# The end of a recurrence and the layer norm behind it, re-ordered over four engines

## The chip, the cores and the metric

The kernel runs on one core of a Trainium2 chip. The metric is the device time of one execution in microseconds (us), as the median of several executions; lower is better. TensorE (PE) does matrix products, VectorE (DVE) and ScalarE (ACT) elementwise work and reductions, GpSimd (POOL) elementwise work on SBUF, and SyncE (SP) starts most DMAs. Each engine works through its own list of instructions in order and waits on semaphores.

## The reference, cut to what matters

The input x has 2048 tokens of width 128. Two blocks follow each other; in each, attention and a feed-forward part read the same layer norm and are added to x.

```python
xn = layernorm(x)
x = x + L0_attn(xn) + L0_ffn(xn)
xn = layernorm(x)                       # the "second norm" of this text
x = x + L1_attn(xn) + L1_ffn(xn)

# L0_attn, F = 64
k, v = phi(k_proj(rmsnorm(xn))), v_proj(rmsnorm(xn))     # phi(z) = elu(z) + 1
for t in tokens:                                          # a recurrence over a 64x128 state M
    M = layernorm_of_matrix(M + eta * norm(v_t - k_t @ M) * outer(k_t, v_t))
out = phi(q_proj(rmsnorm(xn))) @ M @ Wout.T               # only the last M is used

# L0_ffn: expert 1 of the experts, relu(x W1 + b1) W2 + b2
# L1_attn: one head of width 128, the first 64 of them rotated by cos and sin tables, causal softmax
# L1_ffn: ternary weights; silu(x w1) * (x w2), two gelu layers of 512, and w3
```

## The kernel before

The program is written engine by engine; the order on each engine is the order of its code, and every dependence between engines is a semaphore.

**The chain.** The recurrence is cut into 128 lanes of 16 tokens, which start from an assumed state and run 28 steps (the `for j in range(L)` of the VectorE program, L = 28). A step is some seven short VectorE instructions, with a square root on ScalarE in the middle of it (`HS`, then `surprise(j + 1)`). Under it TensorE builds the rest of the first block's output in PSUM banks 0 to 3 (`expert_output(c)` for four blocks of 512 tokens), ScalarE makes copies at fixed steps (`BEHIND_COPY`, `HIDDEN_AT`, `LAST_AT`), and from step 18 VectorE finishes one of the 16 pieces of phi(q) per step (`query_sums`).

**The end of the chain.** TensorE picks a column of the factors (`gcol_done`), VectorE scales the last rows (`UW`), TensorE forms the state times Wout (`mw_done`), ScalarE copies it (`MW`), and `memory_output` adds phi(q) times it to banks 0 to 3. Its last product on a bank raises `ao_done`. Beside this a check compares the end of each lane with the start of the next: `c0` and `c1`, a product that shifts `c0` by one lane, a subtraction, a sum of absolute values, `agree`, a product that counts the lanes that agree, and `flag`. All engines then wait for the flag, load it and branch (`general_path`); a loop over all tokens would follow if lanes did not agree, which is not the case with these inputs.

**The second norm.** It goes by blocks c of 512 tokens. ScalarE copies a block out of PSUM (`first_block`), VectorE takes statistics and variances (block 0 straight from PSUM), ScalarE the square root (`deviations`), VectorE the reciprocal (`shifts`), each of the two normalizes two of the four tiles (`normed`), TensorE transposes (`normed`) and ScalarE copies the result to `xT` (`transposed`). Then `projected` multiplies it with three weights: one to rotate, one swapped, one to skip. VectorE multiplies the first two with the cos and sin tables and adds the halves of the queries; GpSimd adds those of the keys; ScalarE copies the skipped part. The tables are loaded by SyncE, behind a wait for `x1_ready`, into the place of `HT`, which the first block's expert uses until then.

**Behind it** come attention and the gated layer together, tile after tile, then two layers of fp16 products on TensorE, and the stores.

## Time and profile before

| | |
|---|---|
| median of 3 executions | 257.17 us (257.16 to 257.2) |
| the profiled execution | 257.23 us |
| its span, first to last instruction | 255.4 us |
| busy in it | TensorE 244.6, VectorE 204.6, ScalarE 186.1, GpSimd 115.2 us |
| mean granted TensorE clock | 0.997 of full speed |

A time in a row counts from the start of the span. A row of the timeline gives start, duration, engine, line, operation and shapes; neighbours of one line are merged ("x4"), and then the duration is that of the whole run. Durations of neighbours overlap, since an instruction's latency is part of it; the distance between two starts is what it costs the engine. In square brackets stands how long the engine had been idle, and what ended that. "L755" is line 755 of the kernel.

### The profile page before, as it was taken

The page shows a single profiled execution, that of the slowest core. Times are in us where ns is not written, and L with a number is a line of the kernel's source. Part 1 is how long each engine was busy: PE and PEld are TensorE (multiplying, and loading weights), DVE is VectorE, ACT ScalarE, POOL GpSimd, SP SyncE. Part 2 cuts the span into 40 slices and gives each one's busy share as a digit, 9 for nine tenths or more (in the row PEclk, how much of TensorE's full clock was granted, in tenths as well). Part 3 has the DMA queues.
Part 4 walks back from the last instruction along what each step waited for, and adds up shares of the span by engine and source line. Part 5 has one row for each costly group of instructions (what it writes and reads, how often), then busy time and mean ns, then how long its engine had stood idle before and what let it go on. Part 6 is the DMA issues. An engine that isn't in the chain of part 4 may idle for free.

```text
span 255.4 us, 5146 instructions
## 1 busy us (share of the span) xinstructions
PE 244.6 (96%) x1669; PEld 159.9 (63%) x1673; DVE 204.6 (80%) x681; ACT 186.1 (73%) x460; POOL 115.2 (45%) x150
## 2 busy tenths in 40 slices
PE   7899998999998999999999999999999999999993
PEld 2358554776763477787777767886875444444492
DVE  5988799999968998998899887787613996666674
ACT  2597789976637887887767899989814997777720
POOL 9689700000004589887755995987790000000000
PEclk9999999999999999999999999999999999999998
DMA  7720000000007403000000000000000000000014
GB/s 194 209 54 3 1 3 0 1 0 3 3 3 305 190 13 154 3 1 0 4 0 3 0 0 3 1 1 3 1 3 0 0 0 0 3 1 0 1 31 138
DMA packets 8303, 8.50 MB, mean 33 GB/s; under 512 B 1745, under 2 KB 7378, under 8 KB 7762
## 3 DMA queue, kind: packets, MB, share of 16 engines
q1 hardware_dynamic: 7442, 7.65, 9.2%
q10 hardware_dynamic: 832, 0.49, 0.7%
q8 instruction: 15, 0.25, 0.4%
q14 instruction: 14, 0.11, 0.1%
HBM read 7.09 MB, written 1.05 MB: 32 GB/s over the span
## 4 chain that ended last, share of the span: by engine, by line
PE 65%; DVE 19%; POOL 6%; ACT 3%; issue 3%; DMA 2%; DVEq 0%; SPq 0%; POOLq 0%; ACTq 0%
PE PS L954 11%; PE PS L953 11%; PE PS L926 8%; PE PS L903 7%; PE PS L916 4%; POOL arena L1492 3%; POOL arena L1493 3%; PE PS L715 3%; PE PS L669 2%; PE PS L723 2%; DVE mxb L2016 2%; DMA x<-L_attn_x 2%; DVE arena L2002 2%; PE PS L534 2%; PE PS L572 2%
## 5 line engine op out<-in xcount | busy, mean ns | idle before, releaser
L953 PE MATMUL PS<-arena 128*128 128x512 f16 x128 | 48.5, 379 | 0.0
L954 PE MATMUL PS<-arena 128*128 128x512 f16 x128 | 48.5, 379 | 0.0
L2074 DVE TENSOR_TENSOR arena<-arena 128x512 f32<-128x512 f32 x32 | 22.2, 692 | 13.0 <-ACT arena L1411 13.0
L903 PE MATMUL PS<-arena 128*128 128x512 f32 (+3 forms) x80 | 31.9, 530 | 0.3 <-ACT arena L1380 0.3
L1410 ACT ACTIVATE arena<-PS,arena 128x512 f32<-128x512 f32 x32 | 22.9, 716 | 9.1 <-PE PS L954 9.1
L1492 POOL TENSOR_TENSOR arena<-arena 128x256 f32<-128x256 f32 x32 | 21.6, 674 | 15.5 <-DVE arena L2008 13.0
L1380 ACT ACTIVATE arena<-PS,lnt 128x512 f32<-128x512 f32 (+3 forms) x40 | 24.8, 628 | 2.9 <-DVE lnt L2023 2.8
L1493 POOL TENSOR_TENSOR arena<-arena,small 128x256 f16<-128x256 f32 (+1 forms) x36 | 23.8, 662 | 2.8
L1500 POOL CAST arena<-arena 128x512 f16<-128x512 f32 x2 | 1.3, 636 | 49.1 <-ACT x L1273 49.1
L1411 ACT ACTIVATE arena<-PS,arena 128x512 f16<-128x512 f32 x32 | 22.8, 713 | 0.0
L2016 DVE TENSOR_REDUCE mxb<-PS 128x1 f32<-128x512 f32 (+3 forms) x40 | 22.1, 602 | 0.0
L954 PEld LDWEIGHTS PS<-arena 128*128 128x128 f16 x128 | 12.5, 98 | 14.7
L953 PEld LDWEIGHTS PS<-arena 128*128 128x128 f16 x128 | 12.5, 98 | 14.6
L903 PEld LDWEIGHTS PS<-arena 128*128 128x128 f32 x80 | 14.0, 191 | 12.0 <-issue 9.8
L916 PE MATMUL PS<-con,arena 128*128 128x128 f32 x136 | 19.5, 273 | 0.0
L926 PE MATMUL PS<-arena,xn 128*128 128x128 f32 x144 | 19.3, 278 | 0.0
L926 PEld LDWEIGHTS PS<-arena,xn 128*128 128x128 f32 x144 | 17.7, 191 | 1.1 <-ACT xn L1364 0.2
L926 PE MATMUL PS<-arena 128*128 128x128 f32 x128 | 17.3, 278 | 0.6 <-ACT arena L1364 0.6
L916 PEld LDWEIGHTS PS<-con,arena 128*128 128x128 f32 x136 | 15.1, 141 | 2.7 <-issue 1.9
L2045 DVE SCALAR_TENSOR_TENSOR x<-PS,lnt,x 128x128 f32<-128x128 f32 x16 | 5.6, 351 | 13.9 <-PE PS L926 13.6
L926 PEld LDWEIGHTS PS<-arena 128*128 128x128 f32 x128 | 15.6, 191 | 1.3 <-ACT arena L1364 1.0
L2002 DVE SCALAR_TENSOR_TENSOR arena<-PS,arena 128x256 f32<-128x256 f32 x32 | 15.5, 484 | 1.1
(292 smaller groups left out, 614.3 us busy)
## 6 DMA issues: line engine op xcount, KB each, us to landing
arena<-h_T SPq DMA_DIRECT2D x2, 1024.0 KB, 6.0
x<-L_attn_x SPq DMA_DIRECT2D x4, 256.0 KB, 4.7
arena<-cos SPq DMA_DIRECT2D x1, 1024.0 KB, 4.8
arena<-sin SPq DMA_DIRECT2D x1, 1024.0 KB, 6.9
arena<-w_T SPq DMA_DIRECT2D x3, 256.0 KB, 3.0
out<-arena SPq DMA_DIRECT2D x2, 256.0 KB, 2.2
con<-shape_constants ACTq DMA_DIRECT2D x1, 192.5 KB, 3.5
out<-arena SPq DMA_DIRECT2D x1, 192.0 KB, 2.0
```

What stands on the lines that cost most here:

```text
L903: i = mm(PS[:, k, 0:cnt * P], qT1[:, t * P:(t + 1) * P], kT1[:, c * P:(c + cnt) * P], start=True, stop=not last)
L916: i = tr(PS[:, 4 + gi % 2, (b - c) * P:(b - c + 1) * P], Pr[t % 2][:, b * P:(b + 1) * P], ident)
L926: i = mm(PS[:, 7, (t % 4) * D:(t % 4 + 1) * D], PT[t % 2][:, b * P:(b + 1) * P], V1[:, b, :], start=(b == 0), stop=(b == t))
L953: mm(bank(b), wH[:, k, m * P:(m + 1) * P], sH[:, k, cols], start=(k == 0), stop=False)
L954: i = mm(bank(b), wL[:, k, m * P:(m + 1) * P], sL[:, k, cols], start=False, stop=(k == HT4 - 1))
L1380: f(Pr[t % 2][:, c * P:(c + cnt) * P], PS[:, SCORE_BANK[gi], 0:cnt * P], ACT.Exp, scale=1.0 / D, bias=nbs[:, t:t + 1], accum_out=rsums[:, ...
L1410: f(FP[u % 4], bank(u % 8), ACT.Gelu, scale=s_[:, u % HT4:u % HT4 + 1])
L1411: f(high, bank(u % 8), ACT.Gelu, scale=s_[:, u % HT4:u % HT4 + 1]).then_inc(read, 1)
L1492: o.need(o.did(tt(rest, value, high, ALU.subtract)))
L1493: return tt(low, rest, low_scale.broadcast_to([P, cols]), ALU.mult)
L2016: i = did(v.tensor_reduce(mxb[:, gi:gi + 1], PS[:, SCORE_BANK[gi], 0:cnt * P], AX.X, ALU.max))
L2074: v.tensor_tensor(RP[m], FP[m], high, ALU.subtract).then_inc(rest_ready, 1)
```

## The change

1. *Tables.* cos and sin get places of their own. SyncE starts cos when ScalarE has copied the lanes (`lanes_act` 10), sin when the tables of the chain are built; both stand in its queue ahead of the wait for block 3. The buffers `TURN` move to another place.
2. *Last rows.* `LAST_AT` goes from 15 to 16, and the copy of `WVO` moves from behind the chain to step 19.
3. *The check's first part.* At step 13 VectorE takes a reciprocal and at step 18 it forms twelve columns of `c0`; TensorE shifts them before `expert_output(3)`. The `query_sums` at steps 18 to 26 become eight at steps 19 to 26.
4. *End of the chain.* TensorE no longer runs `keep_warm(4)` at step 25. The check's VectorE instructions come right behind `UW`, and the count product goes ahead of all of `memory_output`.
5. *The last half of the queries.* phi(q) is now min(exp(q), 1) + relu(q). For the second half the two terms are not added; VectorE only clips (`query_steps`, two instructions of 256 columns), and TensorE multiplies each term: 16 products where there were 8.
6. *Second norm.* VectorE takes half the statistics of block c + 1 ahead of `shifts(c)`, and `rotated(0)` ahead of `shifts(3)`. ScalarE's order of `first_block`, `deviations`, `normed`, `transposed` and `skipped` is new: `first_block(2)` comes ahead of `deviations(0)`. TensorE transposes block c + 1 inside `projected(c)`, and a transposition starts when its own tile is ready. GpSimd's addition for the keys starts when VectorE's for the queries is done.
7. *Smaller moves.* Five small VectorE instructions on the scales go from behind the norm to before the chain; ScalarE's copies of the masks go ahead of the branch; `keep_warm` behind the output goes from 4 and 7 products to 2 and none.

```diff
-            sp.wait_ge(x1_ready, 2)
-            for i, n in enumerate(("cos", "sin")):
-                sp.dma_start((cosT, sinT)[i], a[n]).then_inc(tab_in, 16)
+            sp.wait_ge(lanes_act, 10)
+            sp.dma_start(cosT, a["cos"]).then_inc(tab_in, 16)
+            sp.wait_ge(tables_ready, 1)
+            sp.wait_ge(terms_act, 2)
+            sp.dma_start(sinT, a["sin"]).then_inc(tab_in, 16)
...
             def memory_output(two, first, end):
-                    pe.wait_ge(q_ready, 2 * (4 * two + k + 1))
+                    pe.wait_ge(q_ready, 9 + k // 2 if two else 2 * (k + 1))
+                    if two:
+                        for c in (2, 3):
+                            mm(PS[:, c, k * P:(k + 1) * P], QE[h0:h0 + F, part], MW[h0:h0 + F, :], start=False, stop=False)
...
-            for j in range(FAR + 1, L):
-                if j in EO_AT:
-                    expert_output(EO_AT.index(j) + 1)
-                elif EO_AT[-1] + 4 < j < L - 2:
-                    keep_warm(4, 4)
+            for k, j in enumerate(EO_AT):
+                if j == EO_AT[-1]:
+                    pe.wait_ge(c0_ready, 1)
+                    mm(PS[0:W, 5, HALF:HALF + REST], ..., c0[0:W - 1, 0:REST], ...).then_inc(shift_done, 1)
+                expert_output(k + 1)
...
+            pe.wait_ge(guard_ready, 2)
+            mm(PS[0:1, 5, 1:2], agree, ...).then_inc(count_done, 1)
             pe.wait_ge(mw_act, 1)
             memory_output(0, 0, 2)
-            pe.wait_ge(agree_ready, 1)
-            mm(PS[0:1, 5, 1:2], agree, ...).then_inc(count_done, 1)
             memory_output(0, 2, 4)
             memory_output(1, 0, 4)
-            keep_warm(4, 4)
+            keep_warm(2, 4)
             general_path(pe, general)
-            keep_warm(7, 4)
...
+            first_block(1)        # ScalarE
+            first_block(2)
+            deviations(0)
+            first_block(0)
+            normed(0)
+            transposed(0)
+            deviations(1)
+            normed(1)
+            first_block(3)
+            deviations(2)
+            transposed(1)
+            normed(2)
+            deviations(3)
+            skipped(0)
+            transposed(2)
+            normed(3)
+            skipped(1)
+            transposed(3)
...
             for c in range(4):    # GpSimd
-                pool.wait_ge(rope_dve, 2 * c + 2)
+                pool.wait_ge(turned_dve, c + 1)
...
-            query_sums(9, 10)
+            query_steps(0)
             (reciprocal, c0, c1, UW, subtraction, sum, agree)
-            query_sums(11, 12, 13, 14, 15)
+            query_steps(1)
             (flag)
...
             for c in range(4):    # VectorE
+                if c < 3:
+                    statistics(c + 1, 0)
+                else:
+                    rotated(0)
                 shifts(c)
                 normed(c)
                 if c < 3:
-                    statistics(c + 1)
+                    statistics(c + 1, 1)
                     variances(c + 1)
+            rotary_sum(0)
+            rotated(1)
+            rotary_sum(1)
+            for c in range(2, 4):
+                rotated(c)
+                rotary_sum(c)
```

## Rows read from the trace of the kernel before

**Rows 1.** Busy time of each engine by stage; (x) counts instructions.
```profile
core 0: us, PE busy (x) PEld busy (x) DVE busy (x) ACT busy (x) POOL busy (x), PEclk, DMA share, GB/s
...
94.00:115.00 21.00, 20.77 (x152) 16.47 (x152) 18.95 (x54) 16.79 (x49) 18.56 (x24) 1.00 0.15 51
...
133.00:250.00 117.00, 116.59 (x747) 75.58 (x748) 84.78 (x190) 88.46 (x181) 46.72 (x52) 1.00 0.01 4
```

**Rows 2.** Chain that ended last, 71 to 81 us: start, duration, what.
```profile
71.11 0.30 DVE arena L1860
...
73.39 0.16 DVE flag L1876
...
74.70 0.90 DVE st L1933 x4
...
76.04 0.30 ACT lnt L1279
...
79.90 0.79 DVE st L1940 x4
```

**Rows 3.** Timeline of TensorE.
```profile
69.94 0.81 PE L510 MATMUL PS<-warm 128*128 128x512 bf16 x3
70.68 0.28 PE L769 MATMUL PS<-con,arena 128*32 128x1 f32 x4
...
72.52 0.71 PE L755 MATMUL PS<-arena 64*128 64x128 f32 x8 [0.20 <-ACT arena L1253]
...
73.28 1.61 PE L755 MATMUL PS<-arena 64*128 64x128 f32 x24
...
77.78 0.66 PE L825 MATMUL PS<-con,xn 128*128 128x128 f32 x4 [0.41 <-ACT xn L1286]
...
79.52 1.12 PE L834 MATMUL PS<-xT,arena 128*128 128x512 f32 x2 [0.21 <-ACT xT L1290]
80.48 1.02 PE L835 MATMUL PS<-xT,arena 128*128 128x512 f32 x2
...
91.94 1.05 PE L850 MATMUL PS<-arena,xT 128*128 128x128 f32 x8
```

**Rows 4.** Timeline of VectorE.
```profile
27.89 0.19 DVE L1675 TENSOR_TENSOR arena<-arena 128x28 f32<-128x28 f32 x1 [1.24 <-ACT arena L1142]
...
59.44 0.20 DVE L1788 TENSOR_TENSOR_SCAN arena<-arena 128x18 f32<-128x18 f32 x1 [0.18 <-ACT arena L1234]
...
76.37 0.18 DVE L1951 RECIPROCAL lnt<-lnt 128x4 f32<-128x4 f32 x1 [0.36 <-ACT lnt L1279]
...
79.01 0.18 DVE L1951 RECIPROCAL lnt<-lnt 128x4 f32<-128x4 f32 x1 [0.36 <-ACT lnt L1279]
...
84.71 0.16 DVE L1968 TENSOR_SCALAR arena<-arena 128x4 f32<-128x4 f32 x1
...
85.18 0.68 DVE L1982 TENSOR_TENSOR arena<-PS,arena 128x512 f32<-128x512 f32 x1
...
92.61 0.69 DVE L1986 TENSOR_TENSOR arena<-arena 64x512 f32<-64x512 f32 x1
```

**Rows 5.** Two lines of GpSimd: count, duration ns min/median/max, first and last start.
```profile
L1507 POOL TENSOR_TENSOR arena<-arena x4: 1701/1773/1778, 86.6 to 92.7; 64x512 f32<-64x512 f32 x4
...
L1492 POOL TENSOR_TENSOR arena<-xT,arena x4: 1156/1156/1161, 94.6 to 101.8; 128x512 f32<-128x512 f32 x4
```

**Rows 6.** Timeline of ScalarE, in the chain and at the softmax's start.
```profile
58.55 0.22 ACT L1184 ACTIVATE arena<-PS 32x64 f32<-32x64 f32 x1 [0.96 <-PE PS L747]
...
69.53 0.40 ACT L1234 ACTIVATE arena<-arena 128x6 f32<-128x6 f32 x1
...
94.01 0.37 ACT L1380 ACTIVATE arena<-PS,lnt 128x128 f32<-128x128 f32 x1
```

**Rows 7.** The line of the table loads (SyncE's queue).
```profile
L449 SPq DMA_DIRECT2D arena<-sin x1: 433/433/433, 77.2 to 77.2; - x1
...
DMA to landing us min/median/max: 4.8/5.8/6.9
```

**Rows 8.** TensorE's work, granted clock and DMA at the end (columns of rows 1).
```profile
254.00:255.40 1.40, 0.00 (x0) 0.00 (x0) 0.00 (x0) 0.00 (x0) 0.00 (x0) 0.50 0.03 9
```

More of the change, by code:

```diff
@@ L241, in program @@
         assert max(b_at[0], at[0]) <= 44992, (b_at, at)
-        TURN = [hBf[:, T * c:T * c + 2 * BANK].rearrange("p (k t) -> p k t", k=2) for c in range(2)]
+        TURN = [hAf[:, 2 * T + 2 * BANK * c:2 * T + 2 * BANK * (c + 1)].rearrange("p (k t) -> p k t", k=2) for c in range(2)]
         xd = hBf[:, T + 2 * BANK:T + 3 * BANK]
@@ L753, in memory_output @@
                     for c in (2 * two, 2 * two + 1):
                         h0 = F * (c % 2)
-                        i = mm(PS[:, c, k * P:(k + 1) * P], QT[h0:h0 + F, (4 * two + k) * P:(4 * two + k + 1) * P], MW[h0:h0 + F, :], start=False, stop=(k == 3))
+                        i = mm(PS[:, c, k * P:(k + 1) * P], QT[h0:h0 + F, part], MW[h0:h0 + F, :], start=False, stop=(k == 3))
                         if k == 3:
                             i.then_inc(ao_done, 1)
-            for j in range(FAR + 1, L):
+            for k, j in enumerate(EO_AT):
@@ L859, in _ @@
                 projected(c)
-                for n in ((2,), (3,), (), ())[c]:
-                    normed(n)
             values(0)
@@ L1294, in high, with skipped @@
                 f(xH[:, c * BANK:(c + 1) * BANK], xT[:, c * BANK:(c + 1) * BANK], ACT.Copy).then_inc(xh_act, 1)
-            first_block(1)
-            deviations(0)
-            first_block(0)
-            normed(0)
-            first_block(2)
-            deviations(1)
-            transposed(0)
-            first_block(3)
-            normed(1)
-            deviations(2)
-            normed(2)
-            transposed(1)
-            deviations(3)
-            normed(3)
-            transposed(2)
-            f(small[:, 38:39], lnt[:, 0, 12:13], ACT.Tanh)
-            for c in range(4):
+            def skipped(c):
                 b = 4 * ((c + 1) % 2)
@@ L1736, in query_sums @@
                     part = slice(q * P // 2, (q + 1) * P // 2)
-                    v.scalar_tensor_tensor(out=QT[:, part], in0=QE[:, part], scalar=1.0, in1=QT[:, part], op0=ALU.min, op1=ALU.max).then_inc(q_ready, 1)
+                    v.scalar_tensor_tensor(out=QT[:, part], in0=QE[:, part], scalar=1.0, in1=QT[:, part], op0=ALU.min, op1=ALU.add).then_inc(q_ready, 1)
             formed = added = o.n
@@ L1828, in _ @@
                     mean_terms(linear)
+                    dve.wait_ge(h_ready, REST)
+                    v.reciprocal(rh[:, 0:1], HS[:, REST:REST + 1]).then_inc(rh_ready, 1)
                     dve.wait_ge(far_done, FAR)
@@ L1853, in _, with query_steps @@
                     formed = mean_terms(formed)
-            query_sums(9, 10)
+            def query_steps(h):
+                part = slice(BANK + h * ZC, BANK + (h + 1) * ZC)
+                v.tensor_scalar(QE[:, part], QE[:, part], 1.0, None, ALU.min).then_inc(q_ready, 1)
+            query_steps(0)
             dve.wait_ge(h_ready, L)
-            v.reciprocal(rh, HS[:, REST:L + 1:HALF]).then_inc(rh_ready, 1)
+            v.reciprocal(rh[:, 1:2], HS[:, L:L + 1]).then_inc(rh_ready, 1)
+            dve.wait_ge(rh_ready, 2)
@@ L1934, in first_variances, with statistics @@
                 variances(0)
-            def statistics(b):
-                dve.wait_ge(x1_ready, b if b == 1 else b + 1)
-                for n in range(4 * b, 4 * b + 4):
+            def statistics(b, half):
+                dve.wait_ge(x1_ready, (1, 2, 4)[b - 1])
+                for n in range(4 * b + 2 * half, 4 * b + 2 * half + 2):
                     did(v.bn_stats(st[:, n, :], x[:, n, :]))
```

117 lines of the change are left out of this document (62 added, 55 removed).

## The prediction

> **What bounds the kernel now.** I read the chain of waits first: up to 70 us it runs through the recurrence, then through the flag and the second norm, then through GpSimd and VectorE in the attention, and from 132 us through TensorE alone. The busy times by stage [rows 1] say the same. From 133 to 250 us TensorE works 116.59 of 117 us, and nothing there is edited. From 94 to 115 us TensorE (20.77 of 21) and GpSimd (18.56) are both nearly full. So the question is how much earlier the work at 94 us can start. Then I read the timelines of 53 to 98 us, engine by engine.
>
> From 70 to 76 us four waits follow each other [rows 2]: UW at 71.11, `memory_output` at 72.52 [rows 3], the flag at 73.39, and 1.31 us later the first statistics at 74.70, though TensorE had finished block 0 before. Those 1.31 us are VectorE's load of the flag and its branch. The square root of block 0 is at 76.04. From 76.37 to the last rotary addition at 92.61 + 0.69 = 93.30 the path stays on VectorE, with idle times of 0.36 us before the reciprocals of blocks 1 to 3 [rows 4] (the second and third repeat the one at 79.01). TensorE's projections run from 79.52 to 91.94 without a gap [rows 3], a second limit close behind. GpSimd's last addition starts at 92.7 and takes 1.77 [rows 5], to 94.43.
>
> **The change, part by part.**
>
> *Tables.* The load of sin starts at 77.2 and lands 6.9 us later [rows 7], at 84.1. Before, that is hidden, since the first product with a table is at 85.18 [rows 4]. Moved alone it is worth nothing, but `rotated(0)` comes at about 82.5 after the change and would wait 1.6 us without it. The new loads start at about 30 and 34 us and have 40 us of cover. In SyncE's queue they stand ahead of the load of h1 alone, which is not delayed by them. I cost their writes under the chain at 0: VectorE's run of four statistics takes its usual 0.79 us at 79.90 [rows 2], under the old load of sin. Bounds 0 to +0.2 us.
>
> *Scales.* Five instructions from 84.71 to 85.18 leave the path, 0.47 us. Their new place is VectorE's idle 1.24 us before 27.89 [rows 4]; their loads stand at the head of SyncE's queue. Cost there 0; without that cover 0.47.
>
> *In the chain.* ScalarE idles 0.96 us before 58.55 for the last rows [rows 6] and so takes the square root of step 16 some 0.3 us late; VectorE idles 0.18 before the scan at 59.44, step 17 [rows 4]. One step later the rows are there: −0.18. The reciprocal at step 13 costs +0.05 to +0.1, the distance between two such small starts. At step 18 the c0 product takes the place of a query piece. Sum −0.13, bounds −0.2 to +0.2.
>
> *End of the chain.* TensorE runs three recorded warm products from 69.94 and reaches the column pick at 70.68 [rows 3], while its factors were ready at 69.53 + 0.40 = 69.93 [rows 6]. Without them, and with the shift product (0.2 us) ahead of `expert_output(3)`, it picks at about 70.2. VectorE now has a clipping, a reciprocal, c0 and c1 ahead of UW, some 0.8 us behind the last scan, so UW moves only from 71.11 to about 70.8. `memory_output` follows 1.41 us behind UW as before (72.52 − 71.11), at 72.2. The check runs right behind UW: three instructions at some 0.2 us (short ones take 0.16 to 0.22 [rows 4, 6]), agreement at 71.6, count at 71.7, flag at 71.95, released engines at 73.25. `memory_output(0)` is 16 records: eight took 0.71 and 24 took 1.61 us [rows 3], so a record costs about 0.06 and 16 with their tail 1.15. Banks 0 and 1 are ready at 73.4, and the statistics of block 0 start there, 1.3 us earlier.
>
> *Two products.* The second half is 32 records instead of 16, about +0.95 us. Banks 2 and 3 are ready at 72.2 + 47 × 0.0575 + 0.27 = 75.2, where they were ready at 73.28 + 1.61 = 74.89. What does this delay? ScalarE's `first_block(2)` waits for it, and `deviations(0)`, ready at 74.7, is queued behind that wait. The copy costs ScalarE 0.5 us, so the square root runs at 75.8 instead of 76.04 [rows 2]. **Of the 1.3 us gained at the flag only 0.24 are left.** Bounds: records at 0.067 us (1.61 / 24) give 75.65 + 0.6 = 76.25, that is +0.2; 0.4 is the most on the other side.
>
> *Second norm on VectorE.* Before: 93.30 − 76.37 = 16.93 us. Off it go the three idle times (1.08), the scales (0.47) and half the statistics of block 1, done ahead (0.4). I walked both engines forward with durations of these rows and found new idle times: 0.1 for the copy of block 0, 0.23 for the square root of block 1, 0.12 for the copy of block 3. Result 15.43, that is −1.5. Bounds −0.8 (each interleave half filled) and −1.9.
>
> *TensorE.* Block 0's transposition ends at 77.75 instead of 78.44 (ScalarE is not on block 2 then), the copy to xT runs at once instead of behind block 2 and a square root, and the first projection starts at 78.6 instead of 79.52. Twelve projections and three transpositions follow as before, where they filled the 12.42 us from 79.52 to 91.94 (some 0.6 us for a transposition, 0.88 for a product [rows 3]). In my walk ScalarE's copies hold them up by little, and they end at 90.35 instead of 91.94, −1.6. VectorE's last rotation needs the swap of block 3 at 89.5 and comes just then.
>
> *GpSimd.* The old additions take 1.70 to 1.78 us on 64 x 512; a subtraction of 128 x 512 takes 1.16 [rows 5]. The old ones start together with VectorE's addition of two SBUF inputs (0.69 us) and the difference is 0.6. Now they start behind it, beside products that read PSUM. I take 1.16: start 0.65 later, 0.6 shorter, no net cost, and the last ends at 91.55 + 1.2 = 92.75 instead of 94.43, −1.7. The other bound is 1.77 again, which leaves −1.1.
>
> The Trainium skill (GPSIMD Engine Reference, Specifications) says that GpSimd's SBUF interfaces are shared with VectorE and contend with VectorE instructions that have two SBUF inputs. The trace agrees with 1.77 against 1.16. By the rule this wait costs nothing; without it the key additions would end 0.6 later.
>
> *Masks, warm products.* The masks (0.3 us each) lie behind MW's copy and end at 72.6, before ScalarE is released. The fewer warm products save nothing on the path, as TensorE waits until 77.78 anyway [rows 3]; they leave it idle for about 1.3 us at 75.7 to 77.0, where the gap was 0.41.
>
> **Sum at the start of the attention.** VectorE: −0.24 − 1.5 = −1.75. TensorE −1.6. GpSimd −1.7. ScalarE, with both `high` copies now ahead of the first exponential (94.01 [rows 6]), −1.2; it is the least full in the stage that follows (16.79 of 21 us [rows 1]), which takes this up. Everything behind is unedited, so I take the smallest of the three that are full: −1.6. The profiled execution took 257.23, the median 257.17. 257.2 − 1.6 = **255.6 us**.
>
> **Rivals.**
>
> *A. The head of ScalarE's queue costs more.* `first_block(2)` is ready late (76.25 for the square root), and the new idle times on VectorE double. Then −0.2 becomes +0.2, −1.5 becomes −1.0: 257.2 − 0.8 = 256.4. For it speaks that one wait holds all four blocks; against it that even then VectorE has a half block of statistics to fill each gap.
>
> *B. The gain is kept in full and more.* If the c = 0 path through the flag, the shorter chain and the transpositions by tile each reach their better bound, TensorE starts 2.3 us earlier: 254.9.
>
> *C. Attention takes the gain back.* It begins with ScalarE 1.2 early only, or with GpSimd at its other bound (−1.1), and what is full is decided by that one: 257.2 − 0.6 to 1.1, or nothing if another engine's order holds it. About 256.7 to 257.2. Against it: all three start together, and no transfer or fixed time stands in between.
>
> *D. Slower: the clock.* The granted clock is 1.00 in every stage [rows 1] but behind the work: 254 to 255.4 us, without one product and behind others without any, has 0.50, that is 1.2 GHz [rows 8]. The kernel after idles 1.3 us at 75.7 and waits in pieces from 71 to 72.2. If the clock fell there, the projections behind it would take 1.7 us each instead of 0.86. It decides from about two of them on (1.6 us lost); six would give 257.2 − 1.6 + 5.2 = 260.8. Against it: 0.41 us of idle time left the clock at 1.00, and the only fall stands behind a longer stretch without work than this change makes.
>
> The Trainium skill (Advanced Engine Details and Errata, Clock Domains) says that the array is gated to 1.2 GHz when idle. The trace agrees at its end only; no stage before it shows such a fall.
>
> *E. The chain gets longer.* Table writes (+0.2) and the two instructions in it (+0.2), and A on top: 257.3 to 257.5.
>
> **Chances and range.** My forecast with its own range of 255.1 to 256.1: 0.58. A: 0.14. B: 0.08. C: 0.10. D: 0.04. E: 0.06. A measurement of this kernel can tell 0.2%, 0.5 us, from no change. Faster than 256.66: forecast, A, B and a fifth of C, 0.82. Same: most of C and half of E, 0.11. Slower: D and half of E, 0.07. The range from 254.8 to 256.7 takes in A and B and leaves out some 0.18.
>
> **What would show it.** In the profile after: UW near 70.8 and the flag near 71.95; L755's counterpart with 48 records, ending near 75.2; ScalarE's second 512-column copy waiting for it, and the first square root behind that, near 75.8; idle before VectorE's reciprocals under 0.25; the last rotary addition ending near 91.5; GpSimd's key additions at about 1.2 us; TensorE's value products starting near 90.4; granted clock 1.00. It is wrong if a projection stands at a half clock, if the chain's last scan comes later than 70.0, or if the softmax starts 1.6 us earlier and the end does not.

## The result, and the profile after

The kernel after took **260.56 us** (median of 4 executions, 259.16 to 260.63), the kernel before on the same chip 257.17 (257.11 to 257.2): a ratio of 1.0116, 95% interval 1.0103 to 1.013. The change makes the kernel 3.4 us slower where 1.6 us less was forecast. The profiled execution took 260.58 us, its span is 258.8 us.

First the windows of the kernel after around the end of the chain (the columns are start and end, length, busy time and count of each engine, granted clock, DMA share, GB/s):

```profile
core 0: us, PE busy (x) PEld busy (x) DVE busy (x) ACT busy (x) POOL busy (x), PEclk, DMA share, GB/s
...
71.00:72.60 1.60, 1.23 (x8) 0.90 (x8) 1.35 (x9) 0.57 (x3) 0.00 (x0) 1.00 0.00 0
72.60:73.00 0.40, 0.37 (x4) 0.38 (x6) 0.00 (x0) 0.37 (x2) 0.00 (x0) 0.76 0.00 0
73.00:76.00 3.00, 3.00 (x32) 3.00 (x30) 1.36 (x10) 0.60 (x1) 0.00 (x0) 0.50 0.00 0
...
79.00:80.00 1.00, 0.00 (x0) 0.00 (x0) 0.97 (x8) 0.41 (x2) 0.00 (x0) 0.82 0.00 0
80.00:83.00 3.00, 2.57 (x8) 1.81 (x10) 1.10 (x7) 1.13 (x3) 0.00 (x0) 0.50 0.02 5
```

The clock stands at 0.50, that is 1.2 GHz, from 73 to 76 us, in the middle of a stretch in which TensorE is busy 3.00 of 3.00 us, and again from 80 to 83. Before each fall TensorE had worked in pieces (1.23 of 1.60 us) or not at all (79 to 80). The pieces alone don't tell a fall: the kernel before works 1.26 us between 71 and 72.6 and stays at 1.00. The timeline of TensorE in the kernel after:

```profile
70.43 0.28 PE L777 MATMUL PS<-con,arena 128*32 128x1 f32 x4 [0.17 <-ACT arena L1239]
...
72.63 1.95 PE L762 MATMUL PS<-arena 64*128 64x128 f32 x16 [0.27 <-ACT arena L1259]
74.36 0.64 PE L759 MATMUL PS<-arena 64*128 64x128 f32 x4
...
76.81 0.39 PE L762 MATMUL PS<-arena 64*128 64x128 f32 x4
77.36 0.38 PE L512 MATMUL PS<-warm 128*128 128x512 bf16 x1 [0.16 <-issue]
80.21 1.11 PE L832 MATMUL PS<-con,xn 128*128 128x128 f32 x4 [2.47 <-issue]
81.55 1.49 PE L512 MATMUL PS<-warm 128*128 128x512 bf16 x3 [0.22 <-issue]
82.83 1.14 PE L841 MATMUL PS<-xT,arena 128*128 128x512 f32 x2
```

L762 and L759 are `memory_output`. Its 48 records (the trace shows two for a product in f32) run from 72.63 to 77.2, 4.6 us, where 3.0 were forecast: a group of four costs 0.43 us at the half clock and 0.22 at the full one (76.59 to 76.81). Then comes the second surprise. The transposition of block 0 starts at 80.21, and what ended TensorE's 2.47 us of idle time is "issue": no other engine. Behind the product at 77.36 stands the branch around the general path of the recurrence. The profile lists the branch under its own line, one row per engine; first the kernel before, then the kernel after:

```profile
L486 PEldq COMPARE_BRANCH  x1: 367/367/367, 74.7 to 74.7; - x1
```

```profile
L488 PEldq COMPARE_BRANCH  x1: 3617/3617/3617, 76.5 to 76.5; - x1
```

The same instruction, taken the same way, takes TensorE 0.37 us before and 3.62 us after. DMA traffic from 70 to 84 us, by queue (packets, MB, share), again before and then after:

```profile
q8 instruction: 1, 0.02, 0.4%
```

```profile
q8 instruction: 2, 0.03, 1.0%
```

Queue 8 carries code in pieces of 16 KB, and it is TensorE's: two kernels below that lengthen TensorE's program alone (e2, f1) have 16 pieces on it in their traces, where these two have 15. In both kernels a piece starts 1.1 us behind the start of the branch, at 75.9 us before and 77.6 after. The next one comes at 89.8 us before and already at 80.9 after, 0.7 us behind the end of the long branch. In the kernel after nothing but code moves between 70 and 84 us, so no other transfer can be in the way.

VectorE and ScalarE in the kernel after, against [rows 2, 4]:

```profile
70.38 0.20 DVE L1804 TENSOR_TENSOR_SCAN arena<-arena 128x18 f32<-128x18 f32 x1
...
71.29 0.28 DVE L1890 TENSOR_SCALAR arena<-arena,PS 64x128 f32<-64x128 f32 x1
...
72.39 0.15 DVE L1901 TENSOR_SCALAR flag<-PS 1x1 int32<-1x1 f32 x1
74.60 0.89 DVE L1958 BATCH_NORM_STATS2 st<-PS 128x6 f32<-128x128 f32 x4 [2.06 <-PE PS L762]
...
78.05 0.18 DVE L1976 RECIPROCAL lnt<-lnt 128x4 f32<-128x4 f32 x1 [1.77 <-ACT lnt L1287]
...
82.18 0.18 DVE L1976 RECIPROCAL lnt<-lnt 128x4 f32<-128x4 f32 x1 [1.86 <-ACT lnt L1287]
```

```profile
77.23 0.60 ACT L1281 ACTIVATE x<-PS 128x512 f32<-128x512 f32 x1 [1.99 <-PE PS L762]
77.73 0.29 ACT L1287 ACTIVATE lnt<-mv,small 128x4 f32<-128x4 f32 x1
```

ScalarE's copy of bank 2 does wait for the doubled products, and the first square root is queued behind it, at 77.73 instead of the forecast 75.8. The last scan of the chain comes at 70.38; it was at 70.03 before. The update of the first tile of the attention is at 99.95 where it was at 96.78, 3.2 us late, and nothing behind gives this back.

### The profile page after: what moved, and what is told of

It is laid out like the page before. It is cut to its first block, busy times and chain, and to the rows that moved or that the text cites. A ratio compares the mean times of both kernels' runs of the same rounds, so it can differ in the third digit from the quotient of the medians.

```text
span 258.8 us, 5147 instructions
## 1 busy us (share of the span) xinstructions
PE 245.1 (95%) x1674; PEld 162.0 (63%) x1678; DVE 204.4 (79%) x676; ACT 185.8 (72%) x460; POOL 113.0 (44%) x150
## 4 chain that ended last, share of the span: by engine, by line
PE 66%; DVE 24%; ACT 3%; issue 3%; DMA 2%; SPq 0%; DVEq 0%; ACTq 0%
PE PS L958 11%; PE PS L959 11%; PE PS L931 9%; PE PS L908 9%; PE PS L921 5%; DVE arena L1785 3%; DVE arena L2036 2%; DVE arena L1772 2%; DVE arena L2035 2%; DVE arena L1804 2%; DMA x<-L_attn_x 2%; DVE mxb L2050 2%; DVE arena L1813 2%; DVE arena L1873 2%; PE PS L882 2%
## 5 line engine op out<-in xcount | busy, mean ns | idle before, releaser
L1373 ACT ACTIVATE xn<-PS 128x512 f32<-128x512 f32 (+1 forms) x20 | 10.4, 551 | 8.4 <-PE PS L921 8.4
```

## The experiments

Sixteen kernels ran, in four sets; each ratio is against the kernel before on the same chip. A position in TensorE's program, in the text below, is that in each kernel's compiled program, labels left out: a product in f32 is four instructions (the trace shows two products in f32 as x4, and as many weight loads), any other two; a wait is part of the instruction behind it or one of its own, and two waits in a row share one. Where the loaded program begins is not known, so only the distances between kernels count. The expectations count from the kernel's text instead, each wait as one, which gives higher numbers: there the kernel before has the target of its first branch at 1669 and its last branch at 4500, here at 1440 and 3739.

**First set: the clock or the branch?**

*e1.* Warm products put back in the chain.

```diff
+            pe.wait_ge(scan_ready, L - 2)
+            keep_warm(4, 4)
             pe.wait_ge(wvo_act, 1)
```

> The changed kernel with the four warm products back behind expert_output(3) (they ran at step 25 of the chain before). Theory 1 (the first fall of the clock, at 72.6 us, comes from TensorE having too little to do from 70.25 on, because these four are gone): granted clock 1.00 from 72 to 76 us; the 48 records of memory_output take about 2.9 instead of 4.6 us, though they start 0.4 to 0.6 us later; the branch of TensorE (3.6 us in the changed kernel) and the gap behind it stay, and the second fall at 79.5 may stay. About 259.2 us. Rival (the two products per tile of the second half are slow by themselves, whatever the clock): the records stay at 0.1 us and the time is 260.6 or more.

258.82 us (257.21 to 259.59), ratio 1.005 (1.0028 to 1.0072). In the profiled execution (259.53) the clock is 1.00 from 72.6 to 76 and `memory_output` takes 2.95 us as forecast. The branch still takes 3.39 us, and TensorE is idle 2.51 us on "issue". The clock then falls behind it. So four products are enough against the first fall, and it isn't all. Three of the ten executions took 257.21 to 257.43 us at a clock of 0.998 to 1.00; no trace of one is kept.

*e2.* The kernel after with its branch later in the program, by 32 waits, fulfilled already, behind each of two `expert_output`s. These 64 waits were meant as 64 instructions and are 32, since two share one. The trace has 30 of them under the line itself:

```profile
L775 PEldq EVENT_SEMAPHORE  x30: 51/51/51, 59.9 to 65.1; - x30
```

```diff
                 expert_output(k + 1)
+                if k < 2:
+                    for _ in range(32):
+                        pe.wait_ge(scan_ready, j + 1)
```

> The changed kernel with 64 extra waits that are already fulfilled in TensorE's program, 32 each behind expert_output(1) and (2), where its queue is full of work; they move every later instruction of TensorE by 64 places and do nothing else. Theory 2 (TensorE's branch takes 3.6 us because its target lies outside the code that is already loaded; code comes in pieces of 16 KB in the trace): the branch takes about 0.4 us as before, block 0 is transposed at about 79.3 instead of 80.2, the clock does not fall a second time or later, about 258.5 to 259.5 us. Rival (the branch is long because the slow products ahead of it have to drain, or because of the flag): it stays at 3.6 us and the time at 260.6.

257.71 us (256.21 to 260.13), ratio 1.0007 (0.9979 to 1.0036). The profiled execution is the 260.13 one, the slowest of ten: branch 3.04 us where 0.4 was expected, and the last branch, around the network's general path, now 1.79 us instead of 0.35. Four of ten executions took 256.2 to 256.35 at a clock of 0.997 to 1.00. In the profiled one the clock did not fall at 72.6 although no warm product had been put back; it fell at 78.4, behind the branch. Only adding instructions that do nothing made the median 2.9 us faster.

*e3.* Both edits.

> Both edits of the first two. If both theories hold and nothing else went wrong in the prediction, the clock is 1.00 throughout, the branch 0.4 us, and the time 255.6 to 256.2 us. If the prediction's sum for the interleaved norm was wrong too, it stays above 256.7.

258.08 us (257.34 to 258.31), ratio 1.0028 (1.0018 to 1.0038), clock 1.00 throughout. The branch took 1.82 us, hidden behind the wait for block 0. The first projection is at 79.09 and the value products start at 91.46, 0.48 earlier than [rows 3]. The last branch took 1.39 us, 1.06 more than before. This was the first sight of the change at full clock: it is worth 0.5 us at the attention, not 1.6.

*e4.* The kernel before, with 64 waits more (33 instructions) in the part of the general path that is jumped over. Nothing that is executed changes.

```diff
                 for two in range(2):
                     memory_output(two, 0, 4)
+                for _ in range(64):
+                    pe.wait_ge(gmw_act, 2)
```

> The kernel before, with 64 waits added inside TensorE's general path, which is jumped over, so that the branch has 64 instructions more to jump. Theory 2: the branch takes 3.6 us instead of 0.37, from 74.7 to 78.3, the seven warm products behind it run after that, block 0 is transposed about 1 us or more later, 258 to 259.5 us. Rival: nothing that is executed is changed, 257.2 us.

259.01 us (258.08 to 259.89), ratio 1.0066 (1.0041 to 1.0091): code that is never executed costs the kernel before 1.8 us in the median. Three executions took 258.08 to 258.39 us at a clock of 0.995 to 1.00, so about 1.0 more, and three 259.62 to 259.89 at 0.989 to 0.993. TensorE in the profiled one (259.76), timeline and windows:

```profile
74.82 1.04 PE L510 MATMUL PS<-warm 128*128 128x512 bf16 x3
78.24 2.73 PE L510 MATMUL PS<-warm 128*128 128x512 bf16 x6 [2.39 <-DVE xn L1959]
```

```profile
76.00:78.00 2.00, 0.00 (x0) 0.00 (x0) 1.49 (x9) 1.93 (x5) 0.00 (x0) 1.00 0.23 33
78.00:82.00 4.00, 3.76 (x12) 2.06 (x13) 2.62 (x18) 0.65 (x3) 0.00 (x0) 0.57 0.89 358
```

The branch itself reads 364 ns here, yet the warm products right behind it, which wait for nothing, start at 78.24. The profile gives the idle time to VectorE, for which these products don't wait. The clock falls to 0.57 after this gap, as in the kernel after.

The Trainium skill (Runtime: NRT & Kernel Launch, Instruction fetch mechanics) says that code comes in blocks of 16 KiB, 256 instructions, ahead of need, and that a taken branch to code outside a window of two blocks has to wait for a fetch. The 16 KB pieces on queue 8 and the 1.8 us of this run agree with it; that the branch itself reads 364 ns here, and the stall stands behind it, is not in it.

**Second set: a cleaner move of the branch; the warm products; the norm.**

*f1.* As e2, with 64 waits in each place, so 32 instructions there.

> The changed kernel with 128 fulfilled waits (64 behind expert_output(1), 64 behind (2)) in TensorE's program instead of the 64 of the run before, and no warm products put back. Theory 2 refined (the piece of code with the branch's target is loaded only once TensorE's program has crossed into the piece before it; with 64 waits that crossing came in the middle of the branch, with 73 places just ahead of it and the branch took 1.8 us; the second branch at the end then took 1.4 to 1.8 us instead of 0.33): with another 64 places both crossings come a microsecond or more earlier, and both branches take about 0.4 us. Block 0 is then transposed when its tiles are ready (78 us or sooner). Time 256.4 to 257.2 us where the clock holds; some runs still lose the clock. Rival (the length of the branch has nothing to do with the place of the code): 3 us again.

259.38 us (258.79 to 259.82), ratio 1.0088 (1.0074 to 1.0101). The branch fell to 0.93 us, but TensorE now idles 0.95 us ahead of an `expert_output` and 0.99 ahead of the c0 product, so UW came 1.7 us late: 128 waits cost time that the chain has no room for. The means spoiled the measurement. Both branches were expected at 0.4 us; the last took 1.17.

*f2.* The kernel before without its warm products at step 25.

```diff
-                elif EO_AT[-1] + 4 < j < L - 2:
-                    keep_warm(4, 4)
```

> The kernel before without its four warm products at step 25: the one edit alone. The prediction had the column pick 0.5 us earlier and UW 0.3 to 0.45 earlier, so 256.8 us by it. Theory 1 (they carried the clock): the granted clock falls between 72 and 76 us in some or all runs, and the time is 257.2 to 258.5 or scatters.

257.07 us (256.77 to 257.49), ratio 0.9997 (0.9988 to 1.0006). In time those products are worth nothing to the kernel before. But they carry its clock too: without them the mean clock is 0.989 to 0.992 in seven of eleven executions, and with them it is 0.996 or more in all 15 that ran beside. The profiled execution of f2 (256.93 us) shows the fall where the kernel after has it; the first row is that of its windows, the second that of `memory_output`:

```profile
73.00:76.00 3.00, 3.00 (x26) 2.50 (x27) 1.43 (x10) 0.94 (x3) 0.00 (x0) 0.53 0.03 5
72.90 2.72 PE L755 MATMUL PS<-arena 64*128 64x128 f32 x24
```

These 24 records take 2.72 us where they took 1.61 [rows 3]. It costs little in the end: the seven executions have a median of 257.21 us, the four others 256.91. UW comes 0.38 us earlier without the four products (70.73), and block 0's square root, which in this order stands ahead of the copy of bank 2, comes at 75.66 instead of 76.04 [rows 2] in this execution with the fall.

*f3* is f1 with warm products in the gaps:

```diff
-            keep_warm(1, 4)               # behind the column pick
+            keep_warm(3, 4)
...
+            keep_warm(1, 6)               # behind the count
             pe.wait_ge(mw_act, 1)
             memory_output(0, 0, 2)
...
             general_path(pe, general)
+            keep_warm(5, 4)
```

*f4* is f3 with the second norm in the order of before on all engines.

> The kernel of the first run of this group, with warm products put only where TensorE waits: two more behind the column pick, one behind the count, and five behind the branch. Clock 1.00 throughout, both branches 0.4 us; block 0's square root at 75.9 to 76.3, projections from about 78.7, attention 0.7 to 1.0 us earlier than before. Theory 3 (what the interleaved norm really gives is about 1 us, not 1.6, and attention gives 0.2 to 0.5 of it back): 256.2 to 256.7 us. By the prediction's sum it would be 255.6.

> The kernel of the run before with the second norm in the order of the kernel before on all four engines (GpSimd's wait too), and everything else as changed. It shows what part 6 is worth at full clock. By the prediction the interleave is worth 1.5 us on VectorE, so 1.2 to 1.5 us slower than the run before; by theory 3, with TensorE's projections as the bound, 0.5 to 0.9 us slower.

f3: 259.70 us (259.53 to 259.91), ratio 1.01 (1.0084 to 1.0115). f4: 258.88 us (258.8 to 259.5), ratio 1.0075 (1.0061 to 1.0089). Both miss what was expected. Warm products alone brought f1 nothing, since its clock was already near 1.00. The old order was to lose 0.5 us or more; it won by 0.8, but 0.57 of that is the last branch, which took 0.99 us in f3 and 0.42 in f4. An uncontrolled branch spoils a comparison of two orders too.

**Third set: the jump shortened, without a wait.**

*g1.* The kernel after with three of four `expert_output`s and six of eight groups of `memory_output` taken out of TensorE's general path, which these inputs never run.

```diff
-                for c in range(4):
-                    expert_output(c)
-                for two in range(2):
-                    memory_output(two, 0, 4)
+                expert_output(3)
+                for two in range(2):
+                    memory_output(two, 3, 4)
```

> The kernel after, with most of TensorE's share of the general path of the recurrence taken out (one expert_output instead of four and two of its eight groups of memory_output). These inputs never run that path, so all work that is executed is the kernel after's, and only the length of the code that is jumped over changes. Theory 'code place': TensorE's branch takes 3.6 us in the kernel after because its target lies too far on, and about 0.4 us here; TensorE is then back at 77.6, waits for block 0's normalised rows (79.4) and transposes them there instead of at 80.2, 0.8 us earlier; with the half clock at 72.6 to 76 left (no warm product is put back) the time is about 259.5. Rival 'clock alone': the branch takes as long as before, or its length hides nothing, and the time stays at 260.5.

257.82 us (257.42 to 259.65), ratio 1.0038 (1.0019 to 1.0057): 2.7 us back, without touching an executed instruction. Its two branches, and TensorE in the block stage:

```profile
L488 PEldq COMPARE_BRANCH  x1: 364/364/364, 75.4 to 75.4; - x1
...
L499 PEldq COMPARE_BRANCH  x1: 1030/1030/1030, 250.8 to 250.8; - x1
```

```profile
75.94 0.38 PE L512 MATMUL PS<-warm 128*128 128x512 bf16 x1 [0.16 <-issue]
77.52 0.86 PE L831 MATMUL PS<-con,xn 128*128 128x128 f32 x4 [1.20 <-DVE xn L1981]
78.43 0.81 PE L512 MATMUL PS<-warm 128*128 128x512 bf16 x3
79.08 1.11 PE L840 MATMUL PS<-xT,arena 128*128 128x512 f32 x2
```

TensorE waits for the normalised rows now, as it should. The gap of 1.2 us that I had forecast is there, and the clock stays at 1.00 behind it. I had expected the fall at 72.6 to remain. By the mean clock it did in two of nine executions only (0.987 and 0.988, 259.24 and 259.65 us); the seven others took 257.42 to 258.04, median 257.79. Between 71 and 72.6 us the profiled one works the same 1.23 of 1.60 us as the kernel after, and its clock stays at 1.00. Without the four products the fall there comes in a part of the executions, and costs this kernel 1.65 us when it does. Of the 2.7 us that g1 gains, that much is the clock's, which falls ahead of the branch; why it falls so much less often here than in the kernel after is open.

*g2* adds the warm products of f3, *g3* the old order of the norm on top, *g4* is g2 with one product instead of two for the last half of the queries.

```diff
-                    if two:
-                        for c in (2, 3):
-                            mm(PS[:, c, k * P:(k + 1) * P], QE[h0:h0 + F, part], MW[h0:h0 + F, :], start=False, stop=False)
...
-                v.tensor_scalar(QE[:, part], QE[:, part], 1.0, None, ALU.min).then_inc(q_ready, 1)
+                v.scalar_tensor_tensor(out=QT[:, part], in0=QE[:, part], scalar=1.0, in1=QT[:, part], op0=ALU.min, op1=ALU.add).then_inc(q_ready, 1)
```

> As the run with the short jump, and with warm products in TensorE's gaps: two more behind the column pick, one behind the count, five behind the branch. Theory (clock and code place are the whole loss): UW at 71.3, memory_output at full clock, 2.95 us, statistics at 74.1, first projection at about 78.9, clock 1.00 up to the end: 256.4 to 257.0, at or a little below the kernel before. Rival 'the new order of the second norm is slower too': above 257.3, and the old order (next run) below this one by 0.5 or more.

> As the run before it, but with the second norm in the order of the kernel before on all engines (rotary and key additions too). If the new order is worth what its earlier projections show (about 0.5 us at the attention, nothing behind tile 6): 0.0 to 0.5 us slower than the run with the new order. If the 0.8 us by which the old order won in the earlier pair of kernels belongs to the order: 0.5 to 0.8 us faster. If it belonged to where the code of the last branch lies (0.57 us there): equal within 0.3.

> As the run with the short jump and warm products, but the last half of the queries is again one product: VectorE adds and clips two pieces of 256 columns in the two places where it only clipped, and TensorE's 16 extra records go. Banks 2 and 3 are ready 0.9 us earlier, UW 0.1 to 0.15 and the flag 0.2 later. If first_block(2) is what holds the square root: 0.4 to 0.7 us earlier at the square root, and up to 0.3 us in the end, since TensorE's projections and attention limit what is left: 256.2 to 256.8. Rival: the two products cost nothing in the end, same within 0.2.

g2: 257.61 us (257.27 to 257.99), ratio 1.0017 (1.0008 to 1.0026). g3: 257.38 (257.09 to 257.75), ratio 1.0009 (1.0 to 1.0018). g4: 257.15 (255.36 to 257.58), ratio 0.999 (0.9973 to 1.0006). g2 and g4 missed what was expected of them, and g3 came out as its third case said (equal to g2 within 0.3). For the misses there is one reason: the last branch took 0.87, 1.00 and 1.61 us. When the layers begin, g2 is 0.29, g3 0.56 and g4 1.08 us ahead of the kernel before, and the branch takes that back. Two executions of g4 took 255.36 and 255.42.

Over the kernels so far, the position of the last branch, taken modulo 256, sorts its time (one profiled execution of each; that of e2 is its slowest):

| kernel | position | modulo 256 | last branch, us |
|---|---|---|---|
| f2 | 3732 | 148 | 0.33 |
| before | 3739 | 155 | 0.33 |
| e4 | 3772 | 188 | 0.33 |
| after | 3775 | 191 | 0.35 |
| e1 | 3783 | 199 | 0.34 |
| e2 | 3807 | 223 | 1.79 |
| g4 | 3553 | 225 | 1.61 |
| e3 | 3815 | 231 | 1.39 |
| g1 | 3577 | 249 | 1.03 |
| f1 | 3839 | 255 | 1.17 |
| g2 | 3593 | 9 | 0.87 |
| g3 | 3595 | 11 | 1.00 |
| f3 | 3855 | 15 | 0.99 |
| f4 | 3857 | 17 | 0.42 |

From 148 to 199 it is short. At 223 it is at its longest, and it falls with the distance from there, over the end of the 256, to 0.42 at 17.

**Fourth set: both branches where such branches were short.** The positions were used as a rule, counted from the text as in the expectations: target of the first branch at 1669 or less, last branch just under 4500, that of the kernel before. In the compiled programs this made targets of 1428 to 1434 and last branches at 127 to 145 modulo 256.

*h1.* The kernel after with the warm products of f3, and 64 instructions less to jump over.

```diff
-                for two in range(2):
-                    memory_output(two, 0, 4)
+                memory_output(0, 2, 4)
+                memory_output(1, 3, 4)
```

*h2* is the kernel after with the single product of g4 and nothing else. *h3* is h2 with the warm products, *h4* is h3 with the old order of the norm. In these three the general path is whole: the single product itself takes away 32 instructions ahead of the branch and 32 inside.

> The kernel after with its warm products in TensorE's gaps, and 64 instructions less in the part of the general path that is jumped over (three of TensorE's eight groups of memory_output are left there; these inputs never run that path). So both branches of TensorE lie where they lay in kernels in which they were short: the first one's target 1669 instructions into the program, as in the kernel before, the last branch at 4494 (before: 4500). Theory 'code place': 0.36 us for the first branch and about 0.35 for the last, and 257.61 - 0.5 to 0.6 = 257.0 us. Rival 'something else delays the end': the last branch is short and the time stays at 257.6; rival 'the place in the program as counted says nothing': one of the branches takes 0.9 us or more.

> The kernel after with one product for the last half of the queries, nothing else: no warm product is put back, and the general path is whole. The 32 instructions that go from each of the two groups bring the first branch's target to 1651 and the last branch to 4476. Theory: both branches short, banks 2 and 3 ready 0.9 us earlier: 256.0 to 256.5 if the clock stays at 1.00 from 71 to 80, 257 to 258 if it falls there. Rival: the order and the missing warm products are what costs, above 259.

> As the run with the single product, and with warm products in TensorE's gaps (two more behind the column pick, one behind the count, five behind the branch); a whole kernel. First target at 1669, last branch at 4494. In the run with the short jump the same work stood 1.08 us ahead of the kernel before when the layers began and lost 1.3 of it in the last branch. Theory: 257.15 - 1.2 = 255.9 us, clock 1.00. Rival: the last branch is long here too, 257.1.

> As the run before it, but with the second norm in the order of the kernel before. In the pair with the doubled product the old order was 0.23 us faster. If that belongs to the order: 255.7, 0.2 under the new order. If the new order needs banks 2 and 3 early (it does, ScalarE copies bank 2 second): the new order is now the faster one, by up to 0.5.

| kernel | median, us | range | ratio (interval) |
|---|---|---|---|
| h1 | 257.08 | 256.81 to 257.19 | 0.9997 (0.9988 to 1.0006) |
| h2 | 256.06 | 255.84 to 257.09 | 0.9966 (0.9953 to 0.9978) |
| h3 | 256.19 | 255.92 to 256.25 | 0.9959 (0.9946 to 0.9972) |
| h4 | 256.58 | 256.39 to 256.74 | 0.9978 (0.9969 to 0.9987) |

In all four the first branch took 0.37 us and the last 0.32, as the rule said. h1, h2 and h4 came out as expected; h3 was expected at 255.9. Here is h1 at the branches:

```profile
L488 PEldq COMPARE_BRANCH  x1: 373/373/373, 75.2 to 75.2; - x1
...
L499 PEldq COMPARE_BRANCH  x1: 317/317/317, 250.7 to 250.7; - x1
```

h1 is the whole change at full clock with short branches: no difference to the kernel before. h2 is the fastest version found, with nothing left out, 1.1 us under the kernel before and 4.5 under the kernel after. The warm products bring it nothing in the median (h3 against h2), but h2 has one execution in six at a clock of 0.991 and 257.09 us, and h3 none.

## Why the prediction was wrong

The forecast was −1.6 us. The kernel lost 3.4, and 3.5 lie between it and h1. **The steps that failed are two that I had costed at nothing.**

**The clock ("The fewer warm products save nothing on the path", and rival D at 0.04).** Rival D had the right mechanism and nearly the right total (260.8), with the clock's fall put at the wrong place: I looked at the idle 1.3 us behind `memory_output`. In g1 a wait of 1.2 us stands there and the clock stays at 1.00. The fall came earlier, behind the pieces up to 72.6, and held `memory_output` for 4.6 us instead of 2.95, so 1.65; the two low executions of g1 give the same 1.65 from total times. My argument against it, that 0.41 us of idle time had left the clock alone, spoke of one gap, not of a stretch of small ones. That the products of step 25 carried the clock is shown from both sides: put back, the fall is gone (e1); taken out of the kernel before alone, it comes (f2, 0.53 from 73 to 76 us). There it costs 0.3 us at most. It costs 1.65 in the kernel after, where `memory_output` has twice the records for banks 2 and 3 and the square root of block 0 is queued behind the copy of bank 2; that this is the reason for the difference is argued and not run by itself. What tips a given execution is not settled: g1 and e2 do the same work in their traces and keep the clock.

**The branch (in no term of the sum).** I priced VectorE's branch at 1.31 us and never asked what TensorE's costs, since TensorE waits for ScalarE behind it anyway [rows 3]. The change adds 20 instructions ahead of it and 32 to the path it jumps. It then takes 3.25 us more. Of these, 0.8 lie on the path directly (80.21 against rows ready at 79.4), and the clock that falls behind the idle time adds 1.06: from the transposition to the first projection it is 2.62 us in the kernel after and 1.56 in h1. By total times: the kernel after at 260.58 against g1's two executions with the first fall, 259.45, is 1.13, and g1 pays 0.68 more at its last branch, together 1.8. With the 1.65 above that makes 3.45 of the 3.48 us between the kernel after and h1. That code which is never executed is the cause is shown from both sides, by e4 (+1.8 in the kernel before) and g1 (−1.1 at a like first fall). Both edits change the length of the jump and the place of its target together; which of the two counts they don't separate.

**The rest, at full clock: h1 against the forecast.** TensorE and VectorE in h1:

```profile
71.21 0.28 PE L780 MATMUL PS<-arena,con 128*128 128x1 f32 x2
...
72.65 1.16 PE L762 MATMUL PS<-arena 64*128 64x128 f32 x16
...
77.33 0.86 PE L834 MATMUL PS<-con,xn 128*128 128x128 f32 x4
...
78.89 1.11 PE L843 MATMUL PS<-xT,arena 128*128 128x512 f32 x2
...
91.26 1.05 PE L859 MATMUL PS<-arena,xT 128*128 128x128 f32 x8
```

```profile
70.30 0.20 DVE L1806 TENSOR_TENSOR_SCAN arena<-arena 128x18 f32<-128x18 f32 x1
...
71.21 0.28 DVE L1892 TENSOR_SCALAR arena<-arena,PS 64x128 f32<-64x128 f32 x1
...
73.84 0.89 DVE L1960 BATCH_NORM_STATS2 st<-PS 128x6 f32<-128x128 f32 x4 [1.37 <-PE PS L762]
...
76.44 0.18 DVE L1978 RECIPROCAL lnt<-lnt 128x4 f32<-128x4 f32 x1 [0.93 <-ACT lnt L1289]
...
91.48 0.69 DVE L2002 TENSOR_TENSOR arena<-arena 64x512 f32<-64x512 f32 x1
```

- *Chain.* Forecast −0.13, got +0.27 at the last scan (70.30 against 70.03; +0.35 in the kernel after). The late last rows gave −0.15 at their step, as argued, and the reciprocal cost +0.05. But two steps elsewhere, at 48 and 68 us, lost 0.2 us each, and the cause is open: small transfers of code stand there, but in the kernel before too. Among the h kernels the last scan varies from 70.19 to 70.51 with no edit in the chain.
- *Flag.* UW 71.21 for 70.8 and statistics 73.84 for 73.4: both late by the chain's error. The step itself, flag and statistics ahead of the output, was right: 0.86 us gained over [rows 2].
- *Doubled product.* 2.95 us for the 48 records (3.0 forecast). The square root is at 76.12: +0.08 where −0.24 was forecast and +0.2 was the bound. So it takes the whole gain at the flag. Against the single product it costs 1.0 us in the end (h1 against h2, or 0.9 against h3). The step named the wait rightly, and by the trace at hand a reader could have said that this part should be left out.
- *Second norm on VectorE.* From first reciprocal to the end of the last rotary addition 15.73 us; 16.93 before, 15.43 forecast. The last one ends at 92.17, 1.13 us earlier than before. This walk held.
- *TensorE's projections: the failed walk.* 78.89 to 91.26 is 12.37 us where I walked 11.75; before it was 12.42. [Rows 3] showed this stretch without a gap, so only its start could move, and moving transpositions about inside it could gain nothing. The walk's own prices say the same: 12 × 0.88 + 3 × 0.6 = 12.36, which from 78.6 ends at 90.96 and not 90.35, and the last 0.3 is the start. With the start 0.63 earlier, the attention gets 0.7 and not 1.6. This is the mis-sized term, and it is the one that decides there, since TensorE gains least of the three: GpSimd's last addition ends at 93.52, 0.91 earlier than before.
- *Second norm in all.* The new order against the old one: 0.2 us slower with the doubled product (g2 against g3, although g3's last branch is 0.13 longer), 0.4 faster with the single one (h3, h4). It pays when banks 2 and 3 come early.
- *Tables, scales, masks.* Hidden, as costed.

**What attention gives back (rival C).** Of the 0.7 us at its start h1 has 0.08 left in the end. That is the outcome of rival C, to which I had given 0.10. The first of GpSimd's key additions in the kernel after:

```profile
89.34 1.27 POOL L1516 TENSOR_TENSOR arena<-arena 64x512 f32<-64x512 f32 x1 [1.07 <-DVE arena L2000]
```

1.27 us instead of 1.77 [rows 5], near the bound that I took. All three engines do start earlier in h1, and the updates of tiles 0 to 5 come 0.47 us earlier; from tile 6 on it is 0.12. That loss is in one instruction, VectorE's cast of 128 x 256. First the kernel before, VectorE (only these three instructions in this stretch) and GpSimd:

```profile
116.81 0.48 DVE L2002 SCALAR_TENSOR_TENSOR arena<-PS,arena 128x256 f32<-128x256 f32 x1
117.40 0.29 DVE L2008 CAST arena<-arena 128x256 f16<-128x256 f32 x1
117.61 1.28 DVE L2016 TENSOR_REDUCE mxb<-PS 128x1 f32<-128x512 f32 x2
```

```profile
116.88 0.62 POOL L1493 TENSOR_TENSOR arena<-arena,small 128x256 f16<-128x256 f32 x1
117.64 0.67 POOL L1492 TENSOR_TENSOR arena<-arena 128x256 f32<-128x256 f32 x1
```

And h1:

```profile
116.92 0.65 DVE L2044 CAST arena<-arena 128x256 f16<-128x256 f32 x1
```

```profile
116.75 0.67 POOL L1503 TENSOR_TENSOR arena<-arena 128x256 f32<-128x256 f32 x1
```

In the kernel before the cast starts 0.10 us before a GpSimd instruction ends and takes 0.29 us. In h1 it starts 0.48 us earlier, 0.50 before the end of one, and takes 0.65, so that it ends only 0.12 earlier than before. Over the whole trace of the kernel before: ten of its twenty casts start beside no GpSimd instruction and each takes 0.29 us. The other ten start beside one, and each ends 0.14 to 0.19 us behind that instruction's end; so they take 0.29 to 1.17 us, by how much of it was left. Whether a cast is lengthened is thus a matter of where it falls. The Trainium skill (GPSIMD Engine Reference, Specifications) names the SBUF interfaces that the two share. How the other 0.2 us between the start of the attention and tile 0 are lost I have not followed. The rival's mechanism was right, with a place that I had not looked for.

## What to carry to other kernels

A kernel with branches has a cost that no engine's busy time shows: where a branch and its target stand, so how many instructions there are ahead of it and inside the part it jumps. Before judging a change by its total time, compare each engine's branch rows and the instruction queue's transfers in both traces. Then, in a stretch that TensorE fills without a gap, count only what moves its start. And a stretch of small waits ahead of a full one is where to look at the granted clock.

## What the runs showed of the hardware

- A taken branch of TensorE took 0.36 us over 97 skipped instructions (g1) and 3.62 us over 295 (the kernel after), with the same executed work around it. For the first branch the target's position sorts all kernels: short up to 1440, and from 1473 on long, first with the time behind the branch (e4), then in it, 3.62 us at 1492 and falling to 0.91 at 1562. The last branch skips 233 instructions everywhere, and there its own position modulo 256 sorts them, short from 127 to 199. I have no single rule for both.
- The time also varies for one program: ten executions of e2 spread from 256.21 to 260.13 us.
- The clock fell to 0.50 within a stretch in which TensorE was fully busy, at 72.8 us, behind one in which it worked 1.23 of 1.60 us; in g1 the same 1.23 left it at 1.00.
- A fulfilled wait is not free on TensorE: two share one instruction of 51 ns (e2), and 128 of them moved UW by 1.7 us (f1).
- VectorE's cast of 128 x 256 takes 0.29 us alone. One that starts beside a GpSimd instruction on SBUF ends 0.14 to 0.19 us behind that instruction, after up to 1.17 us.
